# Attention kernel: the special keys' maxima of two head pairs taken in one VectorE instruction, in batches 13 to 15

## The reference

```python
q = _split_heads(hidden_states @ w_q, HEADS)
k = _split_heads(text @ w_k, HEADS)
v = _split_heads(text @ w_v, HEADS)
out_text = _sdpa(q, k, v)                                 # 248 keys
k_ip = _split_heads(ip_h @ w_k_ip, HEADS)
v_ip = _split_heads(ip_h @ w_v_ip, HEADS)
out_ip = _merge_heads(_sdpa(q, k_ip, v_ip, mask=mask_ip)) # 8 special keys
out = _merge_heads(out_text) + IP_SCALE * out_ip
out = out @ w_out + b_out + residual
```

## Time and profile before

| | us |
|---|---|
| median of 3 runs | 495.56 (495.08 to 496.01) |
| the profiled execution | 496.2 |
| its span in the trace | 494.4 |

### The profile page before, as it was taken

One profiled execution on the slowest core, in us unless ns is written; L12 is line 12 of the kernel. 1 busy time (PEld: TensorE's weight loads), 2 busy tenths in 40 slices (PEclk: granted clock), 3 DMA queues, 4 the chain that ended last, 5 costly groups with the idle time before them and its releaser, 6 DMA issues.

```text
span 494.4 us, 11046 instructions
## 1 busy us (share of the span) xinstructions
PE 465.5 (94%) x4260; PEld 316.6 (64%) x4260; DVE 391.9 (79%) x709; ACT 277.0 (56%) x357; POOL 156.8 (32%) x250
## 2 busy tenths in 40 slices
PE   5897999999999999999999999999999998899987
PEld 4695765676667766676667666676666764555543
DVE  3843877979888797878969697887969789999833
ACT  4641345765465654556645564746546546666672
POOL 4261030725232321314231330413323231524442
PEclk9999999999999999999999999999999999999999
DMA  8989959687683849567592948847593745483011
GB/s 258 369 280 313 367 186 285 178 272 196 168 297 102 274 140 294 173 205 228 159 334 62 322 148 221 256 138 230 163 335 104 242 159 168 134 269 89 10 56 54
DMA packets 94854, 101.80 MB, mean 206 GB/s; under 512 B 16897, under 2 KB 81041, under 8 KB 94801
## 3 DMA queue, kind: packets, MB, share of 16 engines
q1 hardware_dynamic: 93108, 97.63, 63.3%
q0 software_dynamic: 1408, 3.40, 2.5%
q10 hardware_dynamic: 284, 0.05, 0.1%
HBM read 67.87 MB, written 33.23 MB: 204 GB/s over the span
## 4 chain that ended last, share of the span: by engine, by line
PE 68%; DVE 15%; issue 9%; DMA 3%; POOL 3%; ACT 1%; SPq 1%; POOLq 0%; DVEq 0%
PE pv L904 14%; PE pj L913 10%; PE score_t L889 9%; PE score_q L825 7%; DVE max_cols L669 7%; PE score_q L776 4%; PE score_q L771 4%; PE score_q L777 4%; PE score_q L773 3%; PE score_q L778 3%; PE score_q L772 3%; PE score_q L780 2%; PE score_q L781 2%; DVE qk_out L652 2%; DMA o_all<-in_ctxT 1%
## 5 line engine op out<-in xcount | busy, mean ns | idle before, releaser
L579 ACT ACTIVATE probs<-score_t 128x1024 f32<-128x1024 f32 x155 | 158.4, 1022 | 138.3 <-PE score_t L889 137.7
L669 DVE TENSOR_REDUCE max_cols<-score_q 128x4 fp32r<-128x992 f32 x155 | 182.9, 1180 | 55.0 <-PE score_q L825 54.3
L904 PE MATMUL pv<-probs,v_cur 128*32 128x256 f32 x1920 | 120.2, 383 | 2.2 <-ACT probs L579 2.1
L478 POOL TENSOR_TENSOR o_turned<-o_turned,inv_cols 128x256 f32<-128x256 f32 x80 | 53.9, 674 | 152.0 <-DVE inv_cols L722 152.0
L904 PEld LDWEIGHTS pv<-probs,v_cur 128*32 128x32 f32 x1920 | 54.6, 109 | 40.6 <-issue 3.2
L913 PE MATMUL pj<-wo_sb,o_all 128*128 128x320 f32 x186 | 63.2, 460 | 4.0 <-DVE o_all L727 3.9
L468 POOL TENSOR_TENSOR x_all<-x_all,bias_sb 128x640 f32<-128x640 f32 x16 | 25.0, 1562 | 128.5 <-DMA x_all<-in_x 128.5
L719 DVE STREAM_TRANSPOSE o_turned<-o_all 128x512 f32<-128x512 f32 x80 | 55.7, 696 | 11.2 <-ACT o_all L571 11.0
L571 ACT ACTIVATE o_all<-pv 128x512 f32<-128x512 f32 x80 | 47.8, 598 | 29.4 <-PE pv L904 28.8
L889 PE MATMUL score_t<-q_stack,k_stack 64*128 64x256 f32 x420 | 51.7, 324 | 2.7 <-ACT probs L579 2.7
L889 PEld LDWEIGHTS score_t<-q_stack,k_stack 64*128 64x128 f32 x420 | 31.5, 184 | 35.4 <-issue 30.9
(11 more groups left out here) (175 smaller groups left out, 679.1 us busy)
## 6 DMA issues: line engine op xcount, KB each, us to landing
k_stack<-k_parts SPq DMA_DIRECT2D x33, 320.0 KB, 5.4
q_stack<-q_parts SPq DMA_DIRECT2D x33, 320.0 KB, 5.9
q_parts<-qk_out SPq DMA_DIRECT2D x28, 256.0 KB, 3.0
raw<-in_ctxT SPq DMA_DIRECT2D x13, 512.0 KB, 4.3
k_parts<-qk_out SPq DMA_DIRECT2D x24, 248.0 KB, 5.7
v_stage<-v_rows SPq DMA_DIRECT2D x16, 320.0 KB, 6.1
x_all<-in_x SPq DMA_DIRECT2D x16, 320.0 KB, 5.9
stack<-k_parts SPq DMA_DIRECT2D x15, 320.0 KB, 5.0
```

Source lines behind the costliest of these rows:

```text
L478: pool.tensor_tensor(out, out, inv_cols[:, n % SLOTS, :].unsqueeze(2).broadcast_to([P, 2 * S // 32, DH]), ALU.mult).then_inc(scaled, 1)
L579: nc.scalar.activation(probs[:, slot(t % 2, p), :], key_bank(t, p), ACT.Exp, scale=SCALE)\
L669: nc.vector.tensor_reduce(out=max_cols[:, h, :, at:at + 4:2].rearrange("p t e -> p e t"), in_=both[:, :, :, 0:TEXT], op=ALU.max, axis=AX.X ...
L904: last = mm(pv[32 * t:32 * t + 32, at:at + S], values_of(u, kind, 4 * k + t), probs[:, slot(u, 2 * k + t // 2), a:a + S], start=kind != 1, ...
```

## The change

It concerns batches 13, 14 and 15 only (`b > LAST_HOST + 1`). For pairs 0, 2, 6 and 8, `maxima` issues the text keys' instruction and returns: no instruction for the special keys, and nothing is added to `max_done`. For pairs 1, 3, 7 and 9 the special keys' instruction reads all four banks of `score_q`, takes the maxima of this pair and of the one before, writes eight numbers per partition, and adds 2 to `max_done`. Pairs 4 and 5 are as before.

```diff
+JOINED = (0, 2, 6, 8)
@@ maxima(b, p)
-                nc.vector.tensor_reduce(out=max_cols[:, h, :, at + 1:at + 4:2].rearrange("p t e -> p e t"),
-                                        in_=both[:, :, :, TEXT:KEYS], op=ALU.max, axis=AX.X, negate=True)\
-                    .then_inc(max_done, 1)
+                if b > LAST_HOST + 1 and p in JOINED:
+                    return
+                ends, pairs = both, 1
+                if b > LAST_HOST + 1 and p - 1 in JOINED:
+                    ends, pairs = score_q[:, :].rearrange("p (e t n) -> p e t n", e=4, t=2), 2
+                nc.vector.tensor_reduce(out=max_cols[:, h, :, at + 5 - 4 * pairs:at + 4:2].rearrange("p t e -> p e t"),
+                                        in_=ends[:, :, :, TEXT:KEYS], op=ALU.max, axis=AX.X, negate=True)\
+                    .then_inc(max_done, pairs)
```

## The result

| | median us | runs |
|---|---|---|
| before, beside the changed kernel | 496.38 (494.62 to 499.55) | 21 |
| changed | 499.75 (495.96 to 503.75) | 21 |
| ratio | 1.0063 (1.0045 to 1.0081) | |

The changed kernel is slower by 0.6%, 3.1 us. Slower was forecast with 0.85, by 2.5 us; the time forecast was 498.1 with a range up to 499.4, and 499.75 lies above it. So the direction was right and the range missed. One run of the changed kernel, its profiled one at 503.75 us, is over 1.5% above its fastest; it counts as slow and is left out of the ratio.

What follows compares the result with a forecast made beforehand. TensorE's rows were taken as the bound, VectorE just in time. New waits of 0.9 us in batch 13 and 1.64 in batches 14 and 15, 0 from VectorE's savings, gave 495.56 + 2.5 = 498.1 us, range 496.9 to 499.4.

Steps and rivals of the forecast that it cites:

- The bound: Stages 12 to 14: TensorE's rows carry the chain; VectorE, 95 to 96% busy, meets it just in time.
- The second rival: VectorE is the bound in these 57 us, so its shorter list gives 494.9 or 493.8 us; chance 0.06.
- The joined instruction: VectorE's special-key maxima over four banks, 64 elements: 0.21 us, bounds 0.18 and 0.35 us.
- The third rival: The four-bank instruction costs as much as two, 0.35 us, each gate 0.14 us longer: 499.3 us; chance 0.08.
- The gate: From one q to the next, q2, q4 and q8 wait for the joined instruction behind the preceding pair: 1.93 us.
- cover: Batches 14 and 15, pair 4: q3 to q4 already takes 1.95 us against 1.93, so cost 0.
- the first rival: New waits hidden in TensorE's 0.89 us idle times at k2 and k8: 495.6 us; chance 0.08.
- Batch 13: Stage 12: 1.44 us delay at q2 less 0.71 at transposes, plus 0.23 at pair 8: 0.96, taken as 0.9 us.
- Pair 0's removed instruction: Batch 13, ahead of the tile that q1 waits for: may give back up to 0.09 us.
- The term for batches 14 and 15: Pairs 2 and 8: k starts at 2.27 us instead of 1.86, 0.41 us each, 4 x 0.41 = 1.64 us.
- The base: Median of the kernel before, 495.56 us, to which 2.5 us was added; 0.1 us allowed for its spread.
- One sign: VectorE's waits for TensorE in the three windows would grow from seven to nearly one a pair.

Runs made afterwards that it cites:

- The waits alone: Kernel before with its VectorE instructions kept, but max_done in batches 13 to 15 growing only at pairs 1, 3, 7 and 9, by 2; ratio 1.0073.
- the six joins that should be free of a gate: Against the kernel before, only pairs (2, 3) and (8, 9) joined in batches 13 to 15; ratio 1.0003.
- the second profile of the changed kernel: The changed kernel run again without edit, beside the kernel before; ratio 1.0063, profile span 495.9 us.
- the filled kernels: Unused matmuls ahead of batch 13's q2: changed kernel with three 1.0033, with two 1.0045, 1.0038, 1.0036; batch-13-only kernel with two 1.0004, against before.

## Why the prediction missed, point by point

**The bound, right.** TensorE's rows carry these stages, VectorE only just in time. The waits alone reproduce the loss, and 24 more instructions on VectorE do not, though in stage 12, where TensorE waits for VectorE's transposes, they cost 0.38 us. The second rival, faster because VectorE is full, is refuted by both. The Trainium skill says (page Perfetto Trace Analysis, section Optimizing Scalar/DVE Operations) that grouping can improve throughput if the engine is saturated. No gain showed here at 95% busy: the six joins that should be free of a gate gave 1.0003 and made neither stage shorter.

**The joined instruction, right.** 0.21 us forecast, 0.216 measured, over four banks. The third rival is out.

**The gate, right.** 1.93 us forecast; 1.93 measured for q2 in batch 14 and 1.92 in batch 13. q4 was left alone with its 0.02 us of cover, and the first rival, that the waits are hidden, fails by the 1.18 or 1.19 us for which TensorE now stands still.

**Batch 13, right in the sum, by luck in its parts.** 0.96 us worked out, and 0.92 measured from q1 on. Three rows before (TensorE's k4, k6 and next q0), then rows of the second profile of the changed kernel:

```profile
416.16 0.50 PE L889 MATMUL score_t<-q_stack,k_stack 64*128 64x256 f32 x4
419.98 0.50 PE L889 MATMUL score_t<-q_stack,k_stack 64*128 64x256 f32 x4
428.37 0.50 PE L825 MATMUL score_q<-stack 64*128 64x256 f32 x4
```

```profile
414.97 1.34 PE L919 MATMUL pj<-wo_sb,o_all 128*128 128x320 f32 x4
416.24 0.50 PE L895 MATMUL score_t<-q_stack,k_stack 64*128 64x256 f32 x4
...
420.04 0.50 PE L895 MATMUL score_t<-q_stack,k_stack 64*128 64x256 f32 x4
...
422.48 0.40 PE L831 MATMUL score_q<-k_stack,q_stack 64*128 64x256 f32 x4
422.93 1.20 DVE L670 TENSOR_REDUCE max_cols<-score_q 128x4 fp32r<-128x992 f32 x1 [0.49 <-PE score_q L831]
424.31 0.50 PE L831 MATMUL score_q<-k_stack,q_stack 64*128 64x256 f32 x4
...
428.65 0.51 PE L831 MATMUL score_q<-stack 64*128 64x256 f32 x4
```

Counted from q1, the values' product is 1.45 us late, k4 0.72, k6 0.70, q7 0.70, q8 0.83 and the next q0 0.92. So the first wait for a transpose gave back 0.73 us and the second 0.02, where the prediction took 0.47 and 0.24 off. At pair 8 the gate is 1.83 us and not 1.93, because the text maxima start 0.45 us after a q7 that does not start from idle; it costs 0.13 us, and the slower step behind q8 another 0.09, together the 0.23 forecast for the gate alone. Pair 0's removed instruction gave back 0.10 us, ahead of q1, as the prediction had allowed. With it the batch cost 0.82 us.

**The term for batches 14 and 15, mis-sized.** I took 0.41 us for each of the four gates from the start of k. k did come later by that, but the values' product follows k by 0.34 us (433.02 to 433.36) and not by the 0.43 of the earlier trace rows, since q has now taken the start from idle. I had used that longer step for q2 of batch 13 and forgotten that k2 and k8 lose it. 0.30 each was measured, 1.2 us for 1.64. So all the gates make 2.04 us in the profiles, for the 2.5 of the sum.

**What was left out: the clock.** The prediction's sum ran at the clock of 1.00 that the earlier trace rows show and asked nowhere what a second hole of TensorE in stage 12, close behind the one of 1.08 us, does to it. That is the step of the mechanism that failed. In two profiles the clock was at 0.50 behind the two holes of 0.99 and 1.18 us, and stage 12 took 19.70 and 19.71 us for 18.14. In the mean it is worth about 1 us: the ratio is 3.1 us where the gates make 2.0, and the filled kernels were 1.2 us faster. The Trainium skill says (page Perfetto Trace Analysis, section Matmul Optimizations) that the matmul engine scales its power with its utilisation, so that matmuls should run back to back. The granted clock of those two profiles and the mean clock of the filled kernels, 0.9957 for 0.9932, agree with the advice. The prediction did not weigh it.

**The base, which missed the range together with the clock.** The forecast was laid on a median of three runs, 495.56, while 21 runs of the same kernel gave 496.38, 0.8 us more. A tenth of a microsecond for the spread of a median of three was far too little: one step of the clock alone is 1.1 to 2.1 us. With 2.5 us on 496.38 the forecast would have been 498.9, with a range up to 500.2 that holds 499.75; and without the clock's 1 us the measured time would have lain within the range as it was. So each of the two was needed for the miss. The ratio forecast, 1.005, lies within the measured interval, but by two errors against each other: the gates were put 0.5 us too high and the clock at nothing.

**One sign** was wrong. VectorE's waits for TensorE were to grow from seven to nearly one a pair, of thirty pairs; from 405 to 470 us they are nine, of 4.5 us for the 1.9 of before.

## What to carry to other kernels

Before two small instructions are joined, ask what the first of them releases, and when: an instruction that frees a buffer is worth more than its own 0.1 us, and joining it to one that comes a whole reduction later cost 0.3 us at each gate of stages 13 and 14, and 0.7 us at q2 of stage 12. A joined pair whose first member releases nothing early did no harm here beyond 0.12 us, and on an engine that is nearly full but hardly waited for it gained nothing. And, as far as this case shows, a new hole of a microsecond on TensorE close behind another one should be charged with a chance of the lower clock behind it. Last, a median of three runs is no base for a forecast to a few tenths of a microsecond where one kernel's runs spread over 5 us.

## What the runs showed of the hardware that was not expected

A reduction over four PSUM banks cost no more than its elements: 0.216 us for 64 elements in four banks, 0.177 for 32 in two. The mean clock of executions of one and the same kernel moves in steps of 0.0033, each 1.1 to 2.1 us here. In the profiles of the kernel before and of its relatives the half-clock stretches lie in the first 100 us and at the very end; only with two holes of TensorE of 0.99 and 1.18 us close together did one appear in stage 12. None of the kernels tried beats the one before: one matmul in its own hole gave 0.9999, the joins without a gate 1.0003.
